# Gelu a batch later, and the maximum's scores moved to stand behind the attention's second pass

## The reference, cut to what matters

```python
x = x + attn(layernorm(x))        # 16 heads of 8, one key and value head shared, causal
h = layernorm(x)                  # then RMS norm with gamma -> xn
q   = xn @ wq.T                                # 2 x 8 heads x 64
sim = einsum('pbnhd,hkpd->pbnhk', q, keys)     # 32 keys on either side
sx, ix = top_k(sim[0], 16);  sy, iy = top_k(sim[1], 16)
scores, pk = top_k(sx[..., :, None] + sy[..., None, :], 16)
indices = take(ix * 32 + iy, pk)               # 16 experts of 1024, per head
g = gelu(einsum(xn, table_down[indices])) * softmax(scores)
x = x + einsum(g, table_up[indices])
```

## Time and profile before

| | |
|---|---|
| three runs | 1023.99, 1024.22, 1030.28 us |
| median | 1024.22 us |
| profiled execution | 1024.34 us, its span 1022.4 us |
| DVE busy | 828.1 us (81%) |
| PE busy, weight loads | 757.9 us (74%), 489.0 us (48%) |
| ACT busy | 706.1 us (69%) |
| POOL busy | 636.8 us (62%) |
| mean granted clock of TensorE | 0.885 |

### The profile page before, as it was taken

One profiled execution on the slowest core, in us unless ns is written; L12 is line 12 of the kernel. 1 busy time (PEld: TensorE's weight loads), 2 busy tenths in 40 slices (PEclk: granted clock), 3 DMA queues, 4 the chain that ended last, 5 costly groups with the idle time before them and its releaser, 6 DMA issues.

```text
span 1022.4 us, 21166 instructions
## 1 busy us (share of the span) xinstructions
PE 757.9 (74%) x6019; PEld 489.0 (48%) x6066; DVE 828.1 (81%) x3030; ACT 706.1 (69%) x1040; POOL 636.8 (62%) x371
## 2 busy tenths in 40 slices
PE   3662868787877877787888878777878878777374
PEld 2431535455554645454555545554555546453243
DVE  3314588899888889898988988898998887897987
ACT  1342686878778686868868786868787786858271
POOL 2102159494948768593939678593949486686850
PEclk9786978899898989899998989898998989797676
DMA  5322103021212102020212112030212111000000
GB/s 149 52 27 35 18 9 44 1 42 14 40 16 34 22 9 47 0 51 6 40 16 40 16 21 35 8 48 0 41 15 40 16 29 24 0 12 2 5 1 10
DMA packets 51535, 26.49 MB, mean 26 GB/s; under 512 B 5168, under 2 KB 51120, under 8 KB 51312
## 3 DMA queue, kind: packets, MB, share of 16 engines
q1 hardware_dynamic: 51504, 26.11, 15.6%
HBM read 19.93 MB, written 5.24 MB: 25 GB/s over the span
## 4 chain that ended last, share of the span: by engine, by line
PE 46%; ACT 18%; issue 17%; DVE 15%; SPq 1%; DMA 1%; POOL 1%; ACTq 1%; DVEq 0%; POOLq 0%
DVE prob L947 10%; ACT prob L657 9%; PE misc L1173 7%; PE score L1203 5%; PE score L1153 5%; PE score L1234 5%; PE score L1123 4%; PE misc L1262 3%; PE score L1246 3%; PE score L1155 3%; PE misc L1175 3%; ACT late_scores L552 2%; PE misc L1103 2%; PE score L1126 2%; PE misc L1254 2%
## 5 line engine op out<-in xcount | busy, mean ns | idle before, releaser
L458 POOL TENSOR_TENSOR acc<-acc,prob 128x1024 f32<-128x1024 f32 x186 | 440.5, 2368 | 16.6 <-DVE prob L947 0.5
L947 DVE SCALAR_TENSOR_TENSOR prob<-score,cut,prob 128x1024 f32<-128x1024 f32 x256 | 318.1, 1277 | 50.8 <-ACT prob L657 49.2
L657 ACT ACTIVATE prob<-score,neg_lse,unit 128x1024 f32<-128x1024 f32 x256 | 298.5, 1205 | 29.7 <-PE score L1234 27.3
L1234 PE MATMUL score<-sel,pieces_t 128*128 128x512 f16 x512 | 175.4, 440 | 50.6 <-DVE prob L947 38.0
L569 ACT ACTIVATE probs<-score 128x512 f32<-128x512 f32 x192 | 108.0, 599 | 68.7 <-PE score L1155 66.9
L445 POOL TENSOR_TENSOR pieces<-sim,pieces 128x512 f16<-128x512 f32 x32 | 36.4, 1157 | 177.1 <-ACT pieces L613 177.1
L1234 PEld LDWEIGHTS score<-sel,pieces_t 128*128 128x128 f16 x512 | 44.6, 110 | 116.7 <-DVE prob L947 81.3
L1123 PE MATMUL score<-k_ahead,q_ahead 128*128 128x256 bf16 (+1 forms) x512 | 75.1, 251 | 27.9 <-ACT late_scores L552 10.0
L1155 PE MATMUL score<-cb 128*128 128x256 bf16 (+1 forms) x177 | 56.8, 321 | 48.6 <-DVE prob L947 26.3
L1262 PE MATMUL misc<-sel,ident_h 128*128 128x256 f16 x456 | 88.4, 300 | 0.0
L458 POOL TENSOR_TENSOR acc<-prob 128x1024 f32<-128x1024 f32 x31 | 73.0, 2356 | 13.1 <-DVE prob L947 13.1
(11 more groups left out here) (128 smaller groups left out, 1549.4 us busy)
## 6 DMA issues: line engine op xcount, KB each, us to landing
q_ahead<-q_scratch SPq DMA_DIRECT2D x96, 64.0 KB
q_stack<-q_scratch SPq DMA_DIRECT2D x96, 64.0 KB
q_scratch<-qk_piece SPq DMA_DIRECT2D x16, 192.0 KB, 2.4
xin<-x SPq DMA_DIRECT2D x16, 128.0 KB, 4.4
xres<-x SPq DMA_DIRECT2D x16, 128.0 KB, 5.0
out<-fin SPq DMA_DIRECT2D x16, 128.0 KB, 5.5
k_ahead<-qk_piece SPq DMA_DIRECT2D x96, 4.0 KB
k_stack<-qk_piece SPq DMA_DIRECT2D x96, 4.0 KB
```

The costliest lines, as they stand in the source:

```text
L458: eng.tensor_tensor(acc[:, j, :], so_far, prob[:, j * FH + h, :], ALU.add).then_inc(acc_added, 1)
L657: eng.activation(prob[:, g, :], score[g % BUFS][:, :], ACT.Exp, bias=neg_lse[:, j, h:h + 1], scale=unit[:, :]).then_inc(prob_made, 1)
L947: eng.scalar_tensor_tensor(prob[:, g, :], score[g % BUFS][:, :], cut[:, j, h:h + 1], prob[:, g, :], ALU.is_ge, ALU.mult).then_inc(prob_mas ...
L1234: ins = eng.matmul(score[g % BUFS][:, cols], pieces_t[:, j, h, :], sel[:, cols], start=True, stop=True)
```

## The change

- **Gelu a batch later.** `hidden_units` of batch i-1 now run in round i: eight chunks for the second tile, then eight for the first, one after each step of the second pass, in place of `keep_busy`. Their input, the transposed xn, is kept in a new buffer `xn_kept`. `activate(i - 1)` stands on ACT behind the first pass and `invert_sums`. In round 15, which has no attention, both batch 14 and batch 15 are activated.
- **The first pass** of batch i+2 comes directly behind the second pass of batch i+1, and `weigh_values` is cut into eighths between its steps.
- The piece transposes and both acc transposes stand behind `project_y`. The piece transposes use `misc[0]` alone. The first two pair scores wait for the gates.
- **DVE** does both key selections, the sums and the selection of the first tile in one go, and both gates late, directly ahead of the masks. The broadcast operands of `sum_pairs` go to PSUM for both tiles, that of the first subtraction too, and the cut is computed once for both tiles (`place_cut`), behind the gates.
- **SP** issues the copies of x2 as DMAs, which ACT did before, and one of xn.
- **POOL** makes xn at the head of its round, and adds two heads ahead of the low pieces.

The diff, in the order SP, POOL, ACT, DVE, PE; the removed lines of long lists are those of the functions above:

```diff
+    def age_x2(b):
+        copied = held(eng, every(x2_copied, b))
+        read = held(eng, at(fin_made, b, 0))
+        eng.wait_ge(x2_copied, copied)
+        if later(b):
+            eng.wait_ge(fin_made, read)
+        eng.dma_start(x2_aged[:, :, :], x2_kept[:, :, :]).then_inc(x2_moved, 16)
+    def copy_x2(b):
+        made = held(eng, every(x2_made, b))
+        moved = held(eng, at(x2_moved, b, 0))
+        eng.wait_ge(x2_made, made)
+        if later(b):
+            eng.wait_ge(x2_moved, moved)
+        eng.dma_start(x2_kept[:, :, :], x2[:, :, :]).then_inc(x2_copied, 16)
+    def keep_xn(b):
+        made = held(eng, every(xn_t_made, b))
+        used = held(eng, at(hidden, b, 0))
+        eng.wait_ge(xn_t_made, made)
+        if later(b):
+            eng.wait_ge(hidden, used)
+        eng.dma_start(xn_kept[:, :], xn_t[:, :]).then_inc(xn_kept_in, 16)
...
     def iteration(i, d, f, a, m, p):
+        if d and f:
+            age_x2(i - 1)
         if a:
             load_residual(i + 1)
         if p:
             load_x(i + 3)
+        if f:
+            copy_x2(i)
+        if a:
+            keep_xn(i)
         if m:
             stack_pieces(i + 2)
             place_max_row(i + 2)
...
     def iteration(i, d, f, a, m, p):
+        if a:
+            make_xn(i + 1)
         if p:
             make_xhat(i + 3)
+        if f:
+            add_head(i, 0, 1)
+            add_head(i, 0, 2)
         if a:
-            make_xn(i + 1)
             sim_low_piece(i + 1, 0)
             sim_low_piece(i + 1, 1)
         if f:
-            add_head(i, 0, 1)
-            add_head(i, 0, 2)
             add_head(i, 0, 3)
         if p:
             qk_low_piece(i + 3)
...
         if later(b):
-            eng.wait_ge(hidden, at(hidden, b, 0))
+            eng.wait_ge(xn_kept_in, at(xn_kept_in, b, 0))
             eng.wait_ge(sim_made, at(sim_made, b, 0))
...
     def activate(b, j):
         if j == 0:
             eng.preload_act_table_set("gelu_and_others")
-        eng.wait_ge(hidden, at(hidden, b, j + 1))
-        if later(b):
-            eng.wait_ge(gated, at(gated, b - 1, j + 1))
+        eng.wait_ge(hidden, at(hidden, b, 2))
         eng.activation(act_t[:, :, j * P:(j + 1) * P], score[j][:, :].rearrange("p (c t) -> p c t", t=P),
                        ACT.Gelu).then_inc(act_made, 1)
         if j == 1:
...
     def iteration(i, d, f, a, m, p):
         if a:
-            for u in range(10):
+            for u in range(MAX_STEPS):
                 att_exp(i + 1, u)
...
+        if m:
+            for u in range(9):
+                max_scores_back(i + 2, u)
+        if f:
+            best_exp(i, 0)
+        if m:
+            for u in range(9, MAX_STEPS):
+                max_scores_back(i + 2, u)
         if a:
             invert_sums(i + 1)
+        if f:
+            log_sum(i, 0)
+        if d and f:
+            activate(i - 1, 0)
+            activate(i - 1, 1)
         if m:
             copy_v(i + 2)
...
+        if f:
+            pieces_back(i, 0)
+            pieces_back(i, 1)
+        if a:
+            xn_back(i + 1)
+        if f and not a:
             activate(i, 0)
             activate(i, 1)
-        if a:
-            xn_back(i + 1)
-        if f:
+        if f:
+            best_exp(i, 1)
             pair_probs(i, 0, 0)
             pair_probs(i, 0, 1)
+            log_sum(i, 1)
         if a:
             sim_back(i + 1, 0)
             sim_back(i + 1, 1)
         if f:
-            best_exp(i, 1)
-        if f:
             pair_probs(i, 0, 2)
         if a:
             sim_high_piece(i + 1, 0)
+        if f:
+            pair_probs(i, 0, 3)
+        if a:
             sim_high_piece(i + 1, 1)
-        if f:
-            log_sum(i, 1)
-            pair_probs(i, 0, 3)
         if p:
             xhat_back(i + 3)
...
+        placed = misc[1][:, 0:FH * 2 * RANKED].rearrange("p (h k) -> p h k", k=2 * RANKED)
+        eng.tensor_copy(placed, tops).then_inc(top_placed, 1)
+        eng.wait_ge(top_placed, at(top_placed, b, j + 1))
+        tops = placed
...
+        first = best[:, j, :, 0:1]
+        if j == 0:
+            first = misc[1][:, FH * 2 * RANKED:FH * (2 * RANKED + 1)].unsqueeze(2)
+            eng.tensor_copy(first, best[:, j, :, 0:1]).then_inc(first_placed, 1)
+            eng.wait_ge(first_placed, every(first_placed, b))
+        eng.tensor_tensor(shifted[:, j, :, :], best[:, j, :, :], first.broadcast_to([P, FH, TOPK]),
                           ALU.subtract).then_inc(shifted_made, 1)
-        value = held(eng, at(pair_step, b, n + 1))
+    def place_cut(b):
+        ends = ranked[:, :, :, TOPK - 1:RANK_Y + RANKED:RANKED]
+        eng.tensor_reduce(size[:, :, :], ends, AX.X, ALU.add,
+                          apply_absolute_value=True).then_inc(size_made, 1)
+        value = held(eng, every(size_made, b))
         eng.wait_ge(setup_dve, 1)
-        eng.wait_ge(pair_step, value)
-        eng.scalar_tensor_tensor(cut[:, j, :], size[:, j, :], -1.5 * float(2 ** -21), best[:, j, :, TOPK - 1],
-                                 ALU.mult, ALU.add).then_inc(pair_step, 1)
+        eng.wait_ge(size_made, value)
+        eng.scalar_tensor_tensor(cut[:, :, :], size[:, :, :], -1.5 * float(2 ** -21), best[:, :, :, TOPK - 1],
+                                 ALU.mult, ALU.add).then_inc(cut_made, 1)
...
     def iteration(i, d, f, a, m, p):
         if f:
             select_keys(i, 0)
+            select_keys(i, 1)
+            sum_pairs(i, 0)
+            select_pairs(i, 0)
+            sum_pairs(i, 1)
+        if f:
+            sum_best(i, 0)
+            select_pairs(i, 1)
+        if a:
+            make_y(i + 1)
+        if m:
+            fold_max(i + 2, 0, 2)
+        if a:
+            make_x2(i + 1)
+        if p:
+            ln1(i + 3)
+        if f:
+            log_sum_exp(i, 0)
+        if m:
+            fold_max(i + 2, 2, 6)
         if d:
             gate(i - 1, 0)
...
             gate(i - 1, 1)
         if f:
...
+            sum_best(i, 1)
+        if f:
+            place_cut(i)
             mask(i, 0, 0)
+            log_sum_exp(i, 1)
             mask(i, 0, 1)
-            sum_best(i, 1)
             mask(i, 0, 2)
             mask(i, 0, 3)
-            log_sum_exp(i, 1)
             mask(i, 0, 4)
             mask(i, 0, 5)
...
+    def weigh_values(b, j, quads, reader, of_batch):
+        if j == 0 and quads[0] == 0:
             eng.wait_ge(v_copied, every(v_copied, b))
             eng.wait_ge(reader, every(reader, of_batch))
             eng.wait_ge(att_probs, at(att_probs, b, 8))
-        else:
+        elif quads[0] == 0:
             eng.wait_ge(att_probs, every(att_probs, b))
-        for m in range(4):
+        for m in quads:
...
-    def hidden_units(b, j):
-        if later(b):
-            eng.wait_ge(gated, at(gated, b - 1, j + 1))
-        for c in range(CH):
+    def hidden_units(b, j, chunks, source):
+        if chunks[0] == 0:
+            if source is xn_kept:
+                eng.wait_ge(prob_masked, at(prob_masked, b, TILES * FH - 2 * j))
+                eng.wait_ge(xn_kept_in, every(xn_kept_in, b))
+            else:
+                eng.wait_ge(gated, at(gated, b - 1, j + 1))
+        for c in chunks:
             ins = eng.matmul(score[j][:, c * P:(c + 1) * P], wdt[:, c * P:(c + 1) * P],
-                             xn_t[:, j * P:(j + 1) * P], start=True, stop=True)
-        ins.then_inc(hidden, 1)
-    def piece_transposes(b, j, reader, of_batch):
+                             source[:, j * P:(j + 1) * P], start=True, stop=True)
+        if chunks[-1] == CH - 1:
+            ins.then_inc(hidden, 1)
+    def piece_transposes(b, j, reader, value):
         eng.wait_ge(sim_kept, every(sim_kept, b))
-        eng.wait_ge(reader, every(reader, of_batch))
+        eng.wait_ge(reader, value)
         eng.wait_ge(sim_low, at(sim_low, b, j + 1))
-        dst = misc[j][:, :].bitcast(FP16)
+        dst = misc[0][:, :].bitcast(FP16)
...
-        if g < 2:
+        if g < 2 and not a:
             eng.wait_ge(act_made, at(act_made, b, g + 1))
+        elif g < 2:
+            if later(b):
+                eng.wait_ge(gated, at(gated, b - 1, g + 1))
...
     def acc_transposes(b, j):
         eng.wait_ge(prob_masked, every(prob_masked, b))
+        eng.wait_ge(act_made, at(act_made, b, j + 1))
...
     def iteration(i, d, f, a, m, p):
         if a:
             eng.wait_ge(max_t_made, every(max_t_made, i + 1))
-            for u in range(6):
+        if a and d:
+            hidden_units(i - 1, 1, range(0, 4), xn_kept)
+        for u in range(MAX_STEPS):
+            if a:
                 scores_for_probs(i + 1, u)
-                keep_busy(misc[0], 2)
+            if d and f:
+                if u < 4 and a:
+                    hidden_units(i - 1, 1, range(4 + u, 5 + u), xn_kept)
+                elif u >= 4 and a:
+                    hidden_units(i - 1, 0, range(u - 4, u - 3), xn_kept)
+        if d and f and not a:
```

(57 more changed lines are left out.)

106 lines of the change are left out of this document (15 added, 91 removed).

## The result

The changed kernel takes 1068.85 us (median of four runs, 1067.46 to 1073.26), the kernel before beside it 1024.11. The ratio is 1.043, 95% interval 1.038 to 1.048: **44.7 us slower**. I had said 1047, 1009 to 1066. The profiled execution has a span of 1068.0 us, against 1022.4, and a mean granted clock of 0.859, against 0.885.

The account below looks back on a forecast made before the run. Two things fix a round: when DVE gets through its list and when ACT reaches the copy of xhat. 1024.3 + 13 x (1.0 + 0.7) + 1.1 = 1047.5, stated as 1047 us, range 1009 to 1066.

Parts of the forecast that it names:

- last attention exponential ends: ACT's twelve attention exponentials end at 508.0; PE's added chunks of hidden units move the step's end to 508.3.
- ninth score of the maximum: On PE, the maximum's scores alternate with weighing the first tile, 0.38 us each; the ninth stands at 515.2.
- DVE's idle time ahead of its sum: DVE is done at 514.3 and waits 1.9 us for the best pairs' exponential, ending at 516.2.
- first gate ends: DVE's list of 13.1 us from 516.2 ends with the first gate at 529.3.
- gate to second exponential: From the first gate's end through PE's scores and transposes to ACT's second exponential: 4.2 us, starting at 533.5.
- a round, at full clock behind the gate: A round up to xhat at 2.4 GHz takes 57.8 us, 1.0 over the mean of 56.8.
- low clock behind the gate, a round: PE work between gate and second scores at 1.2 GHz: 1.7 us in two rounds of five, 0.7 a round.
- start, rounds 0, 14 and 15: Start some 2 us sooner, round 14 gains 1.4, round 15's first exponential 4.5 us later: net +1.1 us.
- my first rival: Low clock between gate and second scores in every round, 3.1 us instead of 0.7: 1079 at most, chance 0.14.
- No fall in the weighing: PE weighs the values at 2.4 GHz in 5.3 us, where it took 7.0 at a mean clock of 0.76.
- its cover: Gelu in its new place is covered by DVE's selections and folds, costing nothing; 4.6 us without that cover.
- The tables' drain: A page adds some 1.4 us per ACT table switch: up to 0.3 us a round, 1051; forecast used 1.28.

Follow-up runs that it names:

- c1: Changed kernel with 22 idle matmuls directly ahead of the first pair scores alone: 1039.30 us, ratio 1.014.
- a3: Changed kernel with ACT's first exponential of the best pairs behind five copies of the maximum's scores instead of nine: 1059.4 us, ratio 1.035.
- b4: Kernel before with only the broadcast operand of the first subtraction copied to PSUM: 1026.65 us, ratio 1.000.
- b1: Kernel before with 20 idle matmuls in the gap ahead of the weighing of the values: 1010.81 us, ratio 0.985.
- c3: Changed kernel with Copy in place of Gelu and without the two table loads (another output): 1073.81 us, ratio 1.046.
- c5: Kernel before with Copy in place of Gelu and without the two table loads (another output): 1002.09 us, ratio 0.976.
- a2: Changed kernel with both gates on DVE directly behind make_x2: 1017.48 us, ratio 0.994.
- c2: Changed kernel with 12 idle matmuls ahead of project_y and 12 ahead of the second piece transposes, last hole open: 1067.49 us, ratio 1.041.
- a6: Changed kernel with both gates directly behind make_x2 and 18 idle matmuls ahead of the projection: 997.09 us, ratio 0.970.
- c4: Changed kernel with both gates directly behind make_x2, 18 idle matmuls ahead of the projection and 12 ahead of project_y: 998.97 us, ratio 0.976.
- a7: Changed kernel with both gates directly behind make_x2 and the first best-pairs exponential behind five score copies instead of nine: 1014.39 us, ratio 0.987.

## Why the prediction was wrong

The order of events came out as forecast, and so did the sign; the size failed in one term. Against the working, in reference time:

| step | forecast | measured |
|---|---|---|
| last attention exponential ends | 508.3 | 508.4 |
| ninth score of the maximum | 515.2 | 516.6 |
| DVE's idle time ahead of its sum | 1.9 | 3.3 |
| first gate ends | 529.3 | 530.3 |
| gate to second exponential | 4.2 at full clock | 4.1 (c1), 7.0 (changed) |
| a round, at full clock behind the gate | +1.0 | +1.0 (c1); a full round +1.2 |
| low clock behind the gate, a round | +0.7 | +2.4 (c1 against changed); a full round +2.7 |
| round 13, counted as a full one | +1.7 | -2.8 |
| start, rounds 0, 14 and 15 | +1.1 | +2.1 |

**The failed step is the price of the low clock behind the gate: "I take 1.7 us, what the fall in the weighing costs now, in two rounds of five: 0.7."** The bounds, 0 and 3.1, held the value. Within them I took a frequency that no row supported, and the size of another fall. Measured is 60.15 - 57.79 = 2.36 us in the mean of rounds 2 to 13: 13 x 1.66 = 21.6 of the 22 us by which I was off. That this fills the gap so neatly is in part luck. In the full rounds the low clock costs 60.8 - 58.1 = 2.7 us, 12 x 2.0 = 24 us more than forecast, and round 13, which I had counted as a thirteenth full round, gives back 4.5. It is my first rival, in its place and by its mechanism; it gave 1079 at most, and I gave it 0.14. (Its 1062 for one fall of 1.7 in each round is a slip: 1024.3 + 13 x 2.7 + 1.1 = 1060.5.) What I held against it, that PE is busy without pause from 500 to 518, was no argument: the clock was still 1.00 at 553, in reference time 528, and it fell within the next 0.2 us, PE idle since 552.5. I had even written down the row that decides, 534 to 539 with a fall at its end, and had not counted how often it repeats: the projection behind that hole takes 1.22 us in every one of the rounds 1 to 12 of the kernel before. The fall whose size I took, in the weighing, comes in every third round only. Both holes stand in every round, so how often the clock falls in one is to be counted in the trace, round by round.

- **The ninth score** is 1.4 us late (by its copy, at 541.43). Alternated, the scores and the eighths of the weighing take 8.1 us up to there, not 6.9. ACT waits 0.56 to 0.86 us for the scores ahead of each of its copies: PE is the slower side.
- **The gate** came 1.0 us late rather than 1.4, as DVE's list behind the sum was 0.3 shorter than summed. The late exponential costs what a3 gave back, 0.9 us a round. c1's +1.0 meets the forecast's +1.0 all the same, by luck: I had taken 0.7 of it from the reference round, which is that much over its mean of 56.8, the mean of c1 has the short round 13 in it, and in the round of c1 that I read the projection's first matmuls took 0.5 us less than I had counted.
- **No fall in the weighing** (the clock is 1.00 from 533.4 to 544.4), subtraction and log-sum near 0.3: as said, and no row read here waits for the copies on SP. That the subtraction's time brought nothing, b4 shows; for the log-sum and the weighing it isn't shown. In the kernel before, a fill of the hole ahead of the weighing is worth 16 us (b1), part of it through the projection; the change removes that hole and opens the one ahead of the gate.
- **Gelu.** I set its cover right (c3) and never priced its old place by itself; c5 gives 1.6 us a round. With the gates first (a2) a round is 0.6 below the kernel before, and the place of the two gates costs 4.0, of wait and clock together: +3.4. Where the other 1.0 of Gelu's 1.6 goes, no run tells.
- **The tables' drain.** The Trainium skill, ScalarE: Activation LUTs, on what ACT_TABLE_LOAD costs, adds some 1.4 us to a switch. The trace of the changed kernel disagrees as that of before did: ACT's row of the log-sum ends at 546.07, a load of 1.28 us stands at 546.09 and Gelu at 547.38, a load at 549.35 and the next activation at 550.65. There is no room for 1.4 us on either side.
- **The ends.** Round 15's first exponential came 27.4 us after its selection, 2.2 more than in the earlier trace rows and not 4.5; the start, up to the load of round 1, took 3.0 more instead of 2 less. That is mostly the same low clock: the key scores of round 0 take 3.75 us too, and in c1, where they take 1.96, this load stands at 156.97, 0.4 us behind the kernel before.

## What to carry to other kernels

When a step is moved late on one engine, price it twice: by the wait of whoever stands behind it, and by the clock of the matmuls that follow the hole. If the trace shows such a fall in one round of a loop, count in how many rounds it stands: here one hole had it in every full round and another in every third. Take the price from the work directly behind the hole. A hole is cheap to test with idle matmuls, and it is best removed by giving the waiting engine its input earlier: here that brought 51 us where the fill brought 30.

## What the runs showed of the chip

Where the low clock stands differs from one order to another, and within a kernel from round to round. Two pieces of work show it in the rounds 1 to 12: the 16 transposes of the sums, 2.0 us at full clock, and the key scores, 1.96.

| | rounds with transposes over 2.4 us | with key scores over 3.4 us | us |
|---|---|---|---|
| changed | 7 of 12 | 12 | 1068.85 |
| c2 | 0 | 12 | 1067.49 |
| c1 | 7 | 0 | 1039.30 |
| a2 | 12 | 0 | 1017.48 |
| a6 | 7 | 0 | 997.09 |
| c4 | 0 | 1 | 998.97 |

Slow transposes cost nothing that these runs can tell (c2 against the changed kernel, c4 against a6), and slow key scores come with 2.7 us more in each full round (changed against c1). The one slow round of c4 takes 56.5 us, the others 54.8. The mean granted clock (0.898 in c1, 0.879 in a2, 0.884 in a7) therefore says little: a2 is 22 us faster than c1 at a lower clock. What counts is whose work stands in the low stretch.
